# One kernel, four edits: query/key slots loaded as stacks, pieces ended in their own step, PSUM banks in pairs in the tail, turned scores ahead of the first piece

## What is computed

```python
# branch 1: time mixing, then channel mixing
time_out = sigmoid(mix @ Wr) * (vmix @ Wo + bo)
x2 = xn + time_out
kc = square(relu(shift(xc) @ Wck)); vc = kc @ Wcv       # 512 -> 2048 -> 512
branch1 = x2 + sigmoid(xc @ Wcr) * vc
# branch 2: attention, then a mixture of experts
q, k, v = rms(xn) @ Wq.T, rms(xn) @ Wk.T, rms(xn) @ Wv.T   # 16 heads of 32
attn = softmax(causal(q k^T / sqrt(32)))
x = xn + (attn @ v) @ Wo.T
y = rms(x); top 2 of 8 experts; expert: down(silu(Wg y) * (Wu y)), width 1024
branch2 = x + weighted sum of the two experts
out = x_in + branch1 + branch2
```

## Time and profile before

| what | value |
|---|---|
| median of 3 runs | 2160.09 us (2159.92 to 2160.28) |
| profiled execution, its own time | 2173.18 us |
| its span | 2171.3 us |
| mean granted PE clock | 0.95 of full speed |
| busy: PE, PEld, DVE, ACT, POOL | 86%, 73%, 54%, 49%, 24% |
| projections | about 269 to 435 us of the span |
| heads | 435.7 to 1344.6 us |
| experts | 1344.6 us to the end |

### The profile page before, as it was taken

The page is one execution under the profiler, slowest core; times in us unless marked ns, Lnnn a source line. Parts: engine busy times, 40 slices in busy tenths (PEclk is TensorE's granted clock), DMA queues, the critical chain, the costliest instruction groups (busy, mean ns, idle before and its releaser), DMA issues. The chain is left out here.

```text
span 2171.3 us, 30573 instructions
## 1 busy us (share of the span) xinstructions
PE 1872.4 (86%) x10866; PEld 1594.3 (73%) x10866; DVE 1172.8 (54%) x1866; ACT 1055.6 (49%) x1758; POOL 524.8 (24%) x560
## 2 busy tenths in 40 slices
PE   3878679938989888989988754999999999999997
PEld 2666468726767766777766533999999999999986
DVE  6887332135667556666565423555555555555553
ACT  4454344223656555565655312555555555555553
POOL 3243200000000100100100151334344443534343
PEclk9989879969999999999999987999999999999999
DMA  4332345486354433743443314666666665756562
GB/s 174 117 116 97 137 173 193 153 275 142 101 144 114 113 105 112 159 123 100 107 112 101 90 25 148 221 203 204 197 208 209 206 214 196 229 202 205 192 193 49
DMA packets 124211, 334.38 MB, mean 154 GB/s; under 512 B 33743, under 2 KB 33743, under 8 KB 109858
## 3 DMA queue, kind: packets, MB, share of 16 engines
q1 hardware_dynamic: 101266, 291.69, 39.1%
q0 software_dynamic: 18272, 33.13, 9.3%
q10 hardware_dynamic: 4592, 8.52, 1.1%
HBM read 270.67 MB, written 75.06 MB: 159 GB/s over the span
## 5 line engine op out<-in xcount | busy, mean ns | idle before, releaser
L48 PE MATMUL bank<-ex_x_hi,ex_w_hi 128*128 128x256 f32 x1472 | 418.9, 285 | 5.2 <-issue 5.2
L50 PE MATMUL bank<-ex_x_hi,ex_w_lo 128*128 128x256 f32 x1472 | 417.2, 283 | 0.0
L49 PE MATMUL bank<-ex_x_lo,ex_w_hi 128*128 128x256 f32 x1472 | 417.2, 283 | 0.0
L1865 DVE TENSOR_TENSOR ex_w_lo<-ex_stage,ex_w_hi 128x2048 fp32r<-128x2048 f32 x138 | 249.9, 1838 | 147.6 <-ACT ex_w_hi L1810 144.6
L48 PEld LDWEIGHTS bank<-ex_x_hi,ex_w_hi 128*128 128x128 f32 x1472 | 282.9, 192 | 8.2 <-issue 5.6
L49 PEld LDWEIGHTS bank<-ex_x_lo,ex_w_hi 128*128 128x128 f32 x1472 | 283.1, 192 | 2.7
L50 PEld LDWEIGHTS bank<-ex_x_hi,ex_w_lo 128*128 128x128 f32 x1472 | 282.9, 192 | 0.0
L1750 POOL TENSOR_TENSOR ex_a_lo<-ex_a,ex_a_hi 128x256 fp32r<-128x256 f32 x184 | 177.6, 986 | 391.6 <-ACT ex_a_hi L1830 391.1
L1825 ACT ACTIVATE ex_gate<-bank 128x256 f32<-128x256 f32 x184 | 70.7, 384 | 240.0 <-PE bank L50 240.0
L1214 ACT ACTIVATE hd_p_full<-bank 128x512 f32<-128x512 f32 (+1 forms) x192 | 94.4, 528 | 140.7 <-PE bank L1506 139.9
L48 PE MATMUL bank<-hd_down_hi,hd_a_hi 128*128 128x512 f32 x256 | 112.1, 438 | 47.7 <-issue 22.8
(11 more groups left out here) (265 smaller groups left out, 4434.4 us busy)
## 6 DMA issues: line engine op xcount, KB each, us to landing
ex_stage<-in_w_moe SPq DMA_DIRECT2D x69, 1536.0 KB, 6.8
first_w<-in_w_moe SPq DMA_DIRECT2D x23, 1536.0 KB, 7.3
hd_raw<-in_w_up SPq DMA_DIRECT2D x64, 256.0 KB, 2.9
hd_raw<-in_w_dn SPq DMA_DIRECT2D x64, 256.0 KB, 2.8
hd_q<-scratch_q_hi SPq DMA_DIRECT2D x128, 64.0 KB, 2.6
hd_k<-scratch_k_hi SPq DMA_DIRECT2D x128, 64.0 KB, 2.5
tm_x_in<-in_x SPq DMA_DIRECT2D x4, 1024.0 KB, 7.5
scratch_xn<-tm_xn SPq DMA_DIRECT2D x4, 1024.0 KB, 5.2
```

The lines of the kernel that those rows point to most:

```text
L48: pe.matmul(out, lhsT=w_hi, rhs=x_hi, start=first, stop=False)
L49: pe.matmul(out, lhsT=w_hi, rhs=x_lo, start=False, stop=False)
L50: return pe.matmul(out, lhsT=w_lo, rhs=x_hi, start=False, stop=last)
L1865: return dve.tensor_tensor(dst, src, hi.bitcast(F32), ALU.subtract)
```

## The change

- **Stacks.** The projections store straight into one HBM tensor `qk` of stacks: for each sequence and part of 32 partitions one DMA per row group, so 8, 4, 8 and 4 DMAs of 256 KB from 32 partitions each for q_hi, q_lo, k_hi and k_lo, 24 per sequence where there were 4; the high parts are stored twice. A slot is one DMA of 96 partitions, 4 KB each, into one tensor `qk`.
- **Start of the heads phase.** The mixing input and the first slot come ahead of most slices in SP's queue; the waits for constants move from the start to the first use.
- **Pieces.** On ACT and DVE the finish of each piece stands right behind its begin. On ACT the ReLU stands ahead of the fresh weights, and the first piece behind the first two parts of `exps`.
- **Waits of sums.** `down` and `proj` wait for each quarter of their operands just before they use it.
- **Tail.** `up` and sum banks alternate between two; the turned rows and the logits move to banks that are then free.
- **PE's step.** `turned` 0 and 1 stand ahead of the step's first piece.

```diff
     def turn_bank(b, j):
-        return psum[7] if b < B - 1 else psum[j]
+        return psum[7] if b < B - 1 else psum[1 + j % 3]
...
+        def up_bank(k):
+            return psum[4] if k >= TAIL and ups_before[k] % 2 else psum[5]
+        def sum_bank(k):
+            return psum[0] if k >= TAIL and sums_before[k] % 2 else psum[6]
...
             def load_slot(g):
-                b, c, row = feature_rows(g)
-                src = slice(row, row + HD)
-                for n, (qs, ks) in enumerate((("q_hi", "k_hi"), ("q_hi", "k_lo"), ("q_lo", "k_hi"))):
-                    at = slice(n * HD, (n + 1) * HD)
-                    sp.dma_start(q2[at, g % SLOTS, :].bitcast(F32), d[qs][b, c, src, :]).then_inc(slot_in[g % SLOTS], 16)
-                    sp.dma_start(k2[at, g % SLOTS, :].bitcast(F32), d[ks][b, c, src, :]).then_inc(slot_in[g % SLOTS], 16)
+                b, c, part = feature_rows(g)
+                sp.dma_start(qk[0:STACK, g % SLOTS, :, :].bitcast(F32), d["qk"][b, part, :, c]).then_inc(slot_in[g % SLOTS], 16)
...
@@ ACT @@
             for s in range(STEPS):
-                for k in late:
-                    finish(k)
-                for k in ks[:1]:
-                    begin(k)
                 if 0 <= i < N:
                     exps(i, 0)
                     exps(i, 1)
                 for k in ks[:1]:
+                    begin(k)
                     finish(k)
...
                 for k in ks[1:]:
                     begin(k)
+                    finish(k)
                 if s % SET == 0 and SET <= s <= N:
                     max_row(s // SET - 1)
-                late = ks[1:]
@@ PE @@
             def down(k, b, c, j):
-                pe.wait_ge(w_lo_ready, slice_at["down", b, c, DEEP - 1] + 1)
-                pe.wait_ge(a_lo_ready, ups_before[k])
-                total(k, lambda q: a_hi[:, q, :], lambda q: a_lo[:, q, :], j)
+                def ready(q):
+                    pe.wait_ge(w_lo_ready, slice_at["down", b, c, q] + 1)
+                    pe.wait_ge(a_lo_ready, ups_before[k] - DEEP + q + 1)
+                total(k, lambda q: a_hi[:, q, :], lambda q: a_lo[:, q, :], j, ready)
...
-            pe.wait_ge(consts_ready, CONSTS)
-            pe.wait_ge(const_in, 32)
             for s in range(STEPS):
                 if s < N:
                     scores(s, 0)
                     scores(s, 1)
+                if 0 <= i < N:
+                    turned(i, 0)
+                    turned(i, 1)
                 for k in ks[:1]:
                     piece(k)
                 if s < N:
                     scores(s, 2)
-                if 0 <= i < N:
-                    turned(i, 0)
-                    turned(i, 1)
                 if 1 <= i <= N:
                     head_output(i - 1)
@@ projections, SP @@
-            def features_out(name, src, b, out):
-                sp.dma_start(d[name][b].rearrange("c p s -> p c s"), src[:, :, :].bitcast(F32)).then_inc(out, 16)
+            def features_out(src, which, groups, b, out):
+                for part in range(HC):
+                    for g in groups:
+                        sp.dma_start(d["qk"][b, part, g * HD:(g + 1) * HD, :, which, :],
+                                     src[part * HD:(part + 1) * HD, :, :].bitcast(F32)).then_inc(out, 16)
```

124 lines of the change are left out of this document (67 added, 57 removed).

## The result

The changed kernel is **slower** by 0.8%: median 2178.94 us (2171.5 to 2184.1, 5 runs) against 2160.09 us for before (2158.37 to 2164.72, 5 runs), ratio 1.0081, interval 1.0055 to 1.0106. The prediction was 2126 us, range 2088 to 2152, with 0.09 for slower. The profiled execution took 2175.66 us; that of before had been 13.1 us over its median.

What follows compares the result with a forecast made beforehand. PE, busy 86%, was taken to bound the kernel through its waits and lower clock in the heads phase's start, steps and tail. Gains less the row of maxima's price (47 + 20 us) and smaller costs summed to -33.8 us: 2126 us, range 2088 to 2152.

Steps and rivals of the forecast that it cites:

- 47 us: Heads-phase steps: PE's added wait for the row of maxima ahead of the turned scores, 47 us over 16 sets.
- 20 us: Behind the row's stalls: some 11 of 16 followed by 9 matmuls at the lower clock, 20 us lost.
- From issue to the matmul behind it took 2.1 us ... I take 2.1: Row of maxima's DMA: latency to its reader, seen as 2.1 and 4.0 us in before, taken as 2.1.
- The small waits: PE's steps: waits on `o` and `p_lo` save 3 us; DVE's round trips ahead of the maxima cost 4 us.
- My slower rival: Row of maxima costs more than all else gives: 30 us more wait, 38 for 20 of clock; 2174 us, chance 0.09.
- The sign I had set: Prediction wrong if the row DMA's wait sums under 25 or over 80 us, or projections show PE gaps.
- The first piece moves by 20.4 us: Start of heads phase: first piece from 466.25 to about 445.8 us, taken whole as -20.4 us.
- Stores: Projections: stacked stores in 32-partition DMAs at 235 GB/s make the phase end 5.0 us later.
- that rival: Projections: stores at 160 GB/s throttle them, end 18 us late instead of 5; 2168 us, chance 0.10 for over 10 us.
- Waits ahead of pieces, -54.6: PE, 500 to 1190 us: issue and down-weight waits -27, waits on `a` -13.6, lower clock behind them -14 us.
- Tail: End of heads phase: sum banks -6.3, `up` banks -7.3 and -1.3, first quarters -8.3; sum -23.2 us.
- POOL's indirect DMAs end 27 us before its first add, so it does not hold this up: Tail: POOL's indirect DMAs, ending 27 us ahead of its adds, were taken not to limit the -23.2 us gain.

Runs made afterwards that it cites:

- turned_back: The changed kernel with the order of before on PE and ACT: piece, third part of scores, then turned 0 and 1; 2120.85 us, 0.9733 of before.
- maxima_early: The changed kernel with PE turning the maxima ahead of the step's first piece and ACT copying the row behind the first two exponentials; 2101.56 us, 0.9644 of before.
- loads_behind_row: The changed kernel with SP waiting for the row of maxima to land before issuing that step's slot and v loads; 1.0015 of before.
- before_pieces: The kernel before with each finish behind its begin, ReLU ahead of the fresh weights, and sums' waits by quarters; 0.9745 of before.
- best: Early-maxima kernel with before's stores and loads, x's copies into the output in steps 7 to 10, mixing input behind first slot; 2101.7 us, 0.9627 of before.
- copies_late: The early-maxima kernel (0.9644) with SP's four copies of x into the output moved from the phase's start to steps 7 to 10; 0.9602 of before.
- indirects_last: The early-maxima kernel (0.9644) with POOL's 32 indirect DMAs moved behind its last adds; 2123.69 us, 0.9714 of before.
- best_gaps: The 0.9627 early-maxima kernel without stacks, plus two POOL clears (3.4 us) between groups of 8 indirect DMAs; 2090.14 us, 0.9579 of before.

## Why the prediction was wrong

The versions split the change into four steps. Each ratio was measured where before takes 2180 to 2185 us:

| step | predicted us | measured us (of 2180) |
|---|---|---|
| stacks and start | -15.4 | +3.7 (1.0017) |
| pieces, quarters, tail | -51.7 | -61.9 (to 0.9733) |
| turned scores ahead, without the row's wait (measured with the row made early) | -30.6 | -19.4 (to 0.9644) |
| wait for the row of maxima and the clock behind it | +63.9 | +89.6 (to 1.0055) |
| sum | -33.8 | +12.0 |

The third step is not clean: turned_back still has 14.8 us of wait for the row, which maxima_early takes away too, so part of the 19.4 us is the row's. No version has the row early and the turned scores in their old place.

- **The step that failed most is the size of the row's price, "47 us" and "20 us".** Mechanism and place were right: one wait in each of 16 sets, ahead of the turned scores. The wait was 62.5 us, and PE's matmuls took 33 us longer at the lower clock.
  - *The wait.* "From issue to the matmul behind it took 2.1 us ... I take 2.1" is the line that failed. It was right for the kernel before, where the DMA's landing took 2.15 us on average over all 16 sets; what failed is carrying it over. In after it takes 3.29 us, 16 x 1.2 = 19 us more, which more than makes up the 15.5 us missing. Loads beside the row do it: with those of slot and v moved behind it the average is 2.24 us (loads_behind_row). The stacks alone, and the pieces alone, each bring some 0.5 us.
  - *The clock.* I counted 99 matmuls of pieces at the lower clock, 20 us. That part came out: the pieces take 359.9 us of PE's time in after and 338.3 us in maxima_early, 21.6 us apart. What I had put at nothing are the matmuls between the stall and the piece and those behind it: turned scores 6.8 us, scores 4.1 us more.
  - *The small waits.* I took 3 us off those on `o` and `p_lo` and put 4 us on the maxima. They grew by 16.3 us together. The stall itself saves some, as I had it: without it, in maxima_early, they are 37.3 us. But the order of the lists brings more of them (21.3 us in turned_back, 17.1 us in before_pieces), which I had not counted.
  - My slower rival named both terms ("always lands as at 711.43 us", "a whole piece at the lower clock") and got 0.09. Its 2174 us is close to the 2179 measured, but in part by luck: it put the row at 77 + 38 us, more than the 62.5 + 33 measured, and kept the 15 us of the start that did not come. The sign I had set (wrong if the wait is under 25 or over 80 us) was too wide to catch a wait of 62.5 us.
- **"The first piece moves by 20.4 us" and the sum's taking it whole.** The first piece did come 12.3 us earlier, near the forecast 15.4. What failed is that the rest was taken to follow. It does not: in before_pieces and turned_back the first piece lies 15 us apart and the last head output 1 us (1144.7 and 1143.8 us); in the seven traces with early maxima the first piece comes at 447 to 457 us and the last head output at 1120 to 1128 us, in no order with it. I had read the first wait, not what stands next in line: a weight slice far back in SP's queue (the timeline of best).
- **Stores.** The phase starts 6.9 us later, predicted 5.0; 232 GB/s, predicted 235. The 7 us that I had worked out from the Trainium skill, page "SBUF — State Buffer", section "Door 1: The DMA port swizzle", was the better figure; its 218 GB/s stands beside 226 GB/s measured while only such stores run. The projections show no gap on PE, so that rival is out.
- **Waits ahead of pieces, -54.6.** The waits named "issue" and on weights went as forecast. But much of the clock's share, 8.3 us, came with the pieces, so the turned scores were worth at most 19 us and not 31.
- **Tail.** -14.9 predicted for the banks, 19 measured. The line "POOL's indirect DMAs end 27 us before its first add, so it does not hold this up" failed in two ways. With the tail shorter they end just as PE does, and 26.9 us of barrier remain. And ACT and DVE are held while they run, which I had seen as 15.6 us without a name and left in the sum.
- **Open:** why the two comparisons of after differ by 5 us (1.0081 and 1.0055, intervals overlap), and how much of the early start an earlier weight slice would keep. That the late slice gives it back is read from the timelines; the one test near it (copies_late) is within the differences between traces.

## What to carry to other kernels

Before you move a reader ahead in a list that runs in order, ask whether its writer can move too: here the row of maxima cost 92 us while it was made at the step's end. Made ahead of the piece as well, it cost nothing that shows, and both moves together gained 19 us. A latency read from the kernel before holds for its queue: 2.15 us on average there, 3.29 us in the changed kernel, whose loads stand closer to the row. Add the clock: stalls of 1.8 to 8.6 us, 62.5 us in all, cost half as much again in slow matmuls, behind the stall at once and not only in the next piece. And an earlier start is worth what the last wait of the first steps lets through, not what the first wait gives up.

## What the runs showed of the hardware

- The reader of a DMA of 8 KB from SBUF to SBUF starts 1.9 us after the issue where little else is moving, and up to 6.8 us after it behind loads that another engine issued up to 2.3 us before. With those loads held back, 14 of 16 are at 1.9 to 2.3 us (loads_behind_row).
- A single stall of 1.78 us with no other gap of PE in the 6 us before it (after, ending at 906.76 us) is followed by matmuls at the lower clock: the granted clock is 0.50 from 909 to 911 us.
- While POOL issues indirect DMAs without a break (32 in 42 us, 0.96 us each), semaphore updates of PE can be late. From the start of the last matmul of an `up` piece or a sum to the instruction that reads it is 0.43 us as a rule; in the held traces it is up to 24 us for an `up` and 26 us for a sum. The matmuls themselves run on time until PE needs a bank back. The last late update comes 3.2 to 4.6 us after the end of POOL's last indirect DMA in each of the eleven traces that have such updates. It happened in every trace with unbroken indirect DMAs beside pieces on two chips (before at 2180 to 2187 us), in one of the first two traces, and in none of four on the chip where before takes 2163 us. It was gone when the indirect DMAs were moved away (indirects_last), and all but 1.3 us of it when POOL left them out for 3.4 us every 8 (best_gaps); one trace each. The cause was not shown. The Trainium skill, page "Runtime: NRT & Kernel Launch", section "Instruction fetch mechanics", says that each sequencer fetches its instructions in blocks by a DMA queue of its own, mostly hidden. The traces speak against that fetch as the cause: each of these waits ends at the recorded update of a semaphore, and maxima_early shows no transfer of an instruction queue from 1177 to 1237 us, around ACT's wait that ends at 1229.75 us.
- DMAs of 32 partitions stored at 192 to 259 GB/s, 226 on average, with the DMA engines 91 to 100% busy (eight windows of 3 us from 411 to 435 us of after), where those of 128 partitions had run at 375 GB/s.
